# Overlapping the front of an attention block with the drain of a scan block, and weight scaling on GpSimd

## The chip, the cores and the metric

The kernel runs on one core of a Trainium2 chip. Its engines are named as in the profile: PE is TensorE (matmuls), ACT is ScalarE, DVE is VectorE, POOL is GpSimd, SP is SyncE, which issues nearly all DMAs. The metric is the device time of one launch in microseconds (us), the median over several runs.

## The reference

The input is 32 sequences of 256 tokens and 128 features. Two blocks follow each other, each a mixer and a feed-forward part with a residual and a layer norm behind either:

```python
x = _layernorm(x + _L0_attn_ref(x, ...))   # block 0: scan
x = _layernorm(x + _L0_ffn_ref(x, ...))
x = _layernorm(x + _L1_attn_ref(x, ...))   # block 1: attention
x = _layernorm(x + _L1_ffn_ref(x, ...))

# block 0's mixer
x_proj, res = split(x @ W_in.T)
xc = silu(conv_b + sum(conv_w[:, k] * xp[:, k:k + L, :] for k in range(4)))
delta = softplus(xc @ W_dt.T + b_dt)
h = exp(delta * A) * h + delta * Bp * xc      # 16 states, over the tokens
x_ssm = sum(h * Cp) + xc * Dp
return x_ssm * silu(res) @ W_out.T

# feed-forward, both blocks: ternary weights, a scale per output
h = silu(_tlin(x, w1_w, w1_s)) * _tlin(x, w2_w, w2_s)
h = gelu(_tlin(h, h1_w, h1_s)); h = gelu(_tlin(h, h2_w, h2_s))
return _tlin(h, w3_w, w3_s)

# block 1's mixer: 16 heads of 64, 4 memory keys and values in front
q = l2norm(q); k = l2norm(k)
dots = einsum('bhid,bhjd->bhij', q, k) * 10
dots = einsum('hg,bgij->bhij', W_pre_th, dots)
dots = where(causal, mask_value, dots)
vk = top_k(dots, 64)[0][..., -1:]
dots = where(dots < vk, mask_value, dots)
attn = einsum('hg,bgij->bhij', W_post_th, softmax(dots))
out = einsum('bhij,bhjd->bhid', attn, v) * head_scale_params
return (out * sigmoid(x @ Wg + bg)) @ Wo
```

## The kernel before

The program has two phases, one function each, and every engine's instructions are written out in one function per engine (`sync`, `tensor`, `scalar`, `vector`, `gpsimd`). Engines wait for each other on semaphores alone; the order on an engine is the order in which the Python loops emit it.

**Block 0** (`mixer_phase`, called first) is a software pipeline over SEQS + 5 = 37 periods. In period p the engines work on the projection, convolution and scan of sequence p and p - 1, the norm of p - 2, the feed-forward input products (w1, w2) and h1 of n = p - 3, h2 of m = p - 4, and w3 with the second norm (`nb`) of l = p - 5. Sixteen states t of a scan are sixteen `tensor_tensor_scan` on DVE (L921), each followed by a sum into y (L931), with other DVE work set between them at numbered t (LATE is 13). When a sequence's second norm is finished SP stores it to `x_mid` in HBM. PE writes h1 as 16 matmuls out of `f_a`, h2 as 16 out of `f_b` (both L363), w3 as 4 out of `f_c` (L400).

The feed-forward weights are ternary, with a scale per output. `scale_ins` (L143) multiplies w1 and w2 (128 x 512 each) and `scale_hidden` (L149) h1 and h2 (128 x 2048 each) by rows of scales. DVE calls them for block 0 (`f0`) in periods 1 and 2 at t = LATE (L995, L1002), and for block 1 (`f1`) in period 34. The scales come in one tile each, `w_f0rows` and `w_f1rows`. SP loads block 0's feed-forward weights (seven DMAs, `weights0_in`) behind the first sequence and block 1's (`weights1_in`) in period 1.

**Block 1** (`attention_phase`) is a pipeline over SEQS + 3 periods of 128 beats, ordered by tables of beats (`PE_K`, `PE_SCORE0`, `PE_PREMIX`, and so on for each engine). For one sequence b: key pieces `k_piece` (four matmuls of 512 columns for two token halves t and two feature halves), their squares on ACT, a reciprocal root of the norms by a guess on ACT and steps on POOL (`Root`), the transposes of the keys (`k_turn`, eight per token half) and their copies on ACT (`k_keep`); query pieces `q_piece`, squares, sums (`q_sum`), the turned norms (`q_turn`), clipped on DVE (`q_clip`), guess on ACT (`q_guess`), steps on POOL. Then the scores: block of queries 0 (`blk` 0, 132 keys wide) in 6 pieces and block 1 (260 keys) in 16, written by PE into three banks and copied by ACT with the query's scale into the tile `SN` (`s_keep`). SP stores `SN` to HBM (`stage`) and reads it back with 8 queries times 16 heads on the partitions into `T8` (`regroup`), because the heads must be mixed by a matmul. PE does that (`premix`, L1403), ACT copies it back (`t_keep`, L1607), POOL masks it (`hide`), and DVE ranks: eight values at a time, MAX8 and MATCH_REPLACE8, until the 64th largest is known. The ranking of one sequence is by far the largest work of DVE, 1.6 of its 3.4 ms.

Four rows of V per sequence belong to the last tokens of it (`tails`): their inputs are loaded together by one DMA into `x_tail` (in the tile `gate`), and two matmuls of 512 columns and two copies make them, ahead of the very first premix.

**Between the blocks** stands a barrier. For the first sequence of block 1 the keys are made in periods 34 and 35 and the queries in 36 and behind the loop, all inside `mixer_phase`. At the end of it PE, ACT, DVE and POOL each wait for `nb.normed` of the last sequence and raise their semaphore of `mixed_end`; each engine begins `attention_phase` by waiting for all four. Behind the barrier POOL clears `T8`, `V2` and the `AT` tiles by memsets, SP loads `x_tail`, and PE and ACT begin period -1 of the tables with the scores of sequence 0, into which the tables set the first premixes and the keys of sequence 1.

## Time and profile before

| | us |
|---|---|
| three runs, median | 3636.32 |
| lowest, highest | 3629.79, 3643.66 |
| the profiled execution | 3643.09 |
| its span in the trace | 3641.8 |

The granted TensorE clock was 0.981 of full over the span. Busy time of each engine, as a share of the span: PE 3402.0 us (93%), DVE 3429.3 (94%), ACT 3094.4 (85%), POOL 1742.1 (48%). The page cuts the span into 40 slices of 91 us: POOL is at 0 tenths for the first nine of them, which are block 0, and DVE is below 9 in four: the first, the two around the end of block 0, and the last. DMA moves 85 GB/s in the tenth slice, the one between the blocks, and 8 to 14 in block 0 behind the first. "Busy" is an average over stages with different limits, so each place that the change touches is read by itself: a window of the trace gives each engine's busy time in a stretch, a timeline gives single instructions with their start, and what ended the idle time before them stands in brackets.

### The profile page before, as it was taken

Reading aid. Unit: us, or ns where it says so; the run is one execution under the profiler, and the core shown is the slowest. Engines: PE = TensorE matmul, PEld = TensorE weight load, DVE = VectorE, ACT = ScalarE, POOL = GpSimd, SP = SyncE. Lnnn points to the kernel's source line nnn. Section 1 sums busy time; section 2 is a strip of 40 time slices with the busy share of each in tenths; the row PEclk is TensorE's granted clock in tenths of the full one; section 3 lists DMA queues with packets and bytes.
Section 4 is the critical chain, followed back from the end, with each engine's and each line's share of the span. In section 5 each row is a group of like instructions: output and inputs, shape, how many; then the busy total and the mean of one; then the engine's idle time right before and its main releaser. Section 6 shows DMA issues by size and latency. Waiting matters only on the chain.

```text
span 3641.8 us, 78829 instructions
## 1 busy us (share of the span) xinstructions
PE 3402.0 (93%) x19351; PEld 2539.4 (70%) x19351; DVE 3429.3 (94%) x18632; ACT 3094.4 (85%) x10837; POOL 1742.1 (48%) x3670
## 2 busy tenths in 40 slices
PE   4999999996999999999999999999999999999987
PEld 2888888873666666666666666666666666676665
DVE  7999999945999999999999999999999999999993
ACT  5888888856899898999999898998889989889863
POOL 0000000004666666666666666666666666666663
PEclk9999999997899999999999999999999999999998
DMA  3000000003222222222222222222222222222210
GB/s 132 11 14 13 13 13 13 10 8 85 68 74 71 76 83 66 65 65 65 67 65 65 73 70 71 74 69 76 77 73 66 65 65 65 67 65 65 73 55 4
DMA packets 254142, 210.76 MB, mean 58 GB/s; under 512 B 78000, under 2 KB 234736, under 8 KB 252912
## 3 DMA queue, kind: packets, MB, share of 16 engines
q1 hardware_dynamic: 253680, 205.70, 18.2%
q8 instruction: 155, 2.54, 0.3%
q14 instruction: 307, 2.51, 0.2%
HBM read 93.97 MB, written 111.67 MB: 56 GB/s over the span
## 4 chain that ended last, share of the span: by engine, by line
PE 64%; DVE 15%; ACT 14%; issue 3%; POOL 2%; DMA 0%; SPq 0%; DVEq 0%; ACTq 0%; POOLq 0%
PE bank L363 12%; PE bank L221 8%; PE bank L1415 5%; DVE W L1807 5%; PE bank L1403 5%; PE bank L1388 4%; DVE last L1829 3%; PE bank L331 3%; PE bank L1446 3%; PE bank L195 3%; PE bank L453 3%; PE bank L1480 3%; ACT SN L1599 3%; PE bank L1460 2%; PE bank L1419 2%
## 5 line engine op out<-in xcount | busy, mean ns | idle before, releaser
L1807 DVE MATCH_REPLACE8 W<-last,W 128x130 f32<-128x130 f32 (+18 forms) x3456 | 871.0, 259 | 0.0
L1829 DVE MAX8 last<-W 128x8 f32<-128x130 f32 (+18 forms) x3456 | 762.0, 261 | 0.1
L1914 POOL TENSOR_SCALAR posts<-post,share 128x128 f32<-128x128 f32 x1024 | 366.0, 379 | 284.2 <-DVE share L1736 279.7
L1583 ACT ACTIVATE T<-T,peak 128x260 f32<-128x260 f32 (+15 forms) x1024 | 410.9, 409 | 4.2 <-POOL T L1965 3.0
L1599 ACT ACTIVATE SN<-bank,rq 128x260 f32<-128x260 f32 (+1 forms) x1024 | 357.9, 424 | 61.4 <-PE bank L1388 59.7
L1403 PE MATMUL bank<-T,pre 128*128 128x40 f32 (+15 forms) x1024 | 366.1, 440 | 14.1 <-ACT T L1607 9.8
L1415 PE MATMUL bank<-posts,T 128*128 128x128 f32 (+7 forms) x2048 | 311.9, 289 | 69.1 <-POOL posts L1914 60.8
L1965 POOL TENSOR_TENSOR T<-T,below 128x520 f32<-128x520 f32 (+12 forms) x416 | 360.8, 884 | 19.9 <-DVE below L1838 4.6
L1415 PEld LDWEIGHTS bank<-posts,T 128*128 128x128 f32 (+7 forms) x2048 | 249.4, 174 | 165.5 <-POOL posts L1914 89.7
L921 DVE TENSOR_TENSOR_SCAN hs<-dA,dx 128x256 f32<-128x256 f32 x512 | 348.5, 681 | 4.7 <-ACT dA L783 1.9
L1930 POOL TENSOR_TENSOR T<-T,w_mask 128x32 f32<-128x32 f32 x512 | 141.2, 279 | 415.9 <-ACT T L1607 413.5
L1388 PE MATMUL bank<-kT,qT 64*128 64x260 f32 (+1 forms) x2048 | 276.6, 374 | 43.2 <-ACT SN L1599 33.5
L522 POOL TENSOR_SCALAR k_sq<-k_sq 128x16 f32<-128x16 f32 x64 | 17.6, 275 | 571.5 <-DVE k_sq L535 522.1
L1403 PEld LDWEIGHTS bank<-T,pre 128*128 128x128 f32 x1024 | 169.5, 193 | 165.6 <-issue 87.0
L1955 POOL TENSOR_SCALAR below<-T,last 128x244 f32<-128x244 f32 (+3 forms) x256 | 269.2, 1051 | 32.3 <-DVE last L1827 8.9
L1807 DVE MATCH_VALUE_LOAD W<-last,W 128x8 f32 x3456 | 260.9, 76 | 0.0
L221 PE MATMUL bank<-f_b,w_f1h 128*128 128x256 f32 x1024 | 248.6, 386 | 5.7 <-ACT f_b L233 5.7
L1607 ACT ACTIVATE T<-bank 128x40 f32<-128x40 f32 (+15 forms) x512 | 208.0, 406 | 50.2 <-PE bank L1403 47.9
L1552 ACT ACT_TABLE_LOAD x192 | 246.3, 1283 | 4.6 <-POOLq L1081 1.1
L221 PE MATMUL bank<-f_a,w_f1h 128*128 128x256 f32 x1024 | 247.7, 385 | 0.0
L783 ACT ACTIVATE dA<-delta,neg_a 128x256 f32<-128x256 f32 x512 | 235.8, 499 | 8.7 <-DVE delta L1048 8.6
L1388 PEld LDWEIGHTS bank<-kT,qT 64*128 64x128 f32 x2048 | 146.8, 191 | 136.7 <-ACT SN L1599 76.1
(243 smaller groups left out, 9571.9 us busy)
## 6 DMA issues: line engine op xcount, KB each, us to landing
scores_by_token<-SN SPq DMA_DIRECT2D x64, 520.0 KB, 3.0
scores_by_token<-SN SPq DMA_DIRECT2D x64, 396.0 KB, 3.6
scores_by_token<-SN SPq DMA_DIRECT2D x32, 780.0 KB, 3.3
scores_by_token<-SN SPq DMA_DIRECT2D x32, 264.0 KB, 2.7
scores_by_token<-SN SPq DMA_DIRECT2D x32, 260.0 KB, 2.3
T<-scores_by_token SPq DMA_DIRECT2D x32, 244.0 KB, 2.9
T<-scores_by_token SPq DMA_DIRECT2D x32, 228.0 KB, 3.1
T<-scores_by_token SPq DMA_DIRECT2D x32, 212.0 KB, 4.0
```

What stands on the lines that cost most here:

```text
L221: last = pe.matmul(o[:, (m % 2) * SEQ:(m % 2 + 1) * SEQ], self.w[layer][:, c, m * P:(m + 1) * P], src[:, c, :], start=c == 0, stop=c == HC ...
L363: last = pe.matmul(o[:, (m % 2) * SEQ:(m % 2 + 1) * SEQ], self.w[layer][:, c, m * P:(m + 1) * P], src[:, c, :], start=c == 0, stop=c == HC ...
L921: dve.tensor_tensor_scan(hs[j % NH][:], dA[j % ND][:], dx[b % 2][:], 0.0, ALU.mult, ALU.add).then_inc(scanned, 1)
L1388: last = pe.matmul(FRONT[(n + half) % 3][:, j * w:(j + 1) * w], qT[rows, even // 2, blk * P:(blk + 1) * P], kT[rows, even // 2, 0:w], star ...
L1403: pe.matmul(MIX[:, 0:pair.shape[-1]], pre[:], pair, start=True, stop=True).then_inc(premixed, 1)
L1415: return pe.matmul(at0[0:m, j * P:(j + 1) * P], scores(b, QUAD[i][j], 0, m), posts[(n + j) % NP][:], start=True, stop=True)
L1583: act.activation(one, one, ACT.Exp, bias=peak[k % 2][:, j:j + 1], accum_out=total[k % 4][:, j:j + 1]).then_inc(e_made, 1)
L1599: last = act.activation(SN[:, h, 0:w], FRONT[n % 3][:, j * w:(j + 1) * w], ACT.Copy, scale=rq[:, c:c + 1])
L1807: dve.match_replace(both[:, s, at:to], best[n], both[:, s, at:to], LOWEST).then_inc(ranked, 1)
L1829: dve.max(best[n], both[:, s, at:to]).then_inc(ranked, 1)
L1914: pool.tensor_scalar(posts[(4 * k + j) % NP][:], post[:], share[k % 2][:, j:j + 1], 1.0, ALU.mult, ALU.mult).then_inc(posts_made, 1)
L1965: pool.tensor_tensor(x, x, out, ALU.add).then_inc(dropped, 1)
```

## The change

Four things are changed.

1. `scale_ins` and `scale_hidden` are called by POOL, for both blocks, one set behind the other at the start of its program, as soon as the weights are in. The scales of both blocks are loaded into parts of `SN`, which is free until block 1; the two tiles for them are gone.
2. Keys and queries of the first sequence are made earlier: the first token half's keys at the end of period 33, the second half's ahead of h1 in period 34, the first half's transposes behind h1 of period 34, the queries in period 35. The scores of sequence 0 follow directly behind the last norm in period 36, all 22 pieces in a row, and SP's store of them likewise. `score`, `s_keep` and `stage` become methods of `Front` for it.
3. The barrier is taken apart: no `mixed_end`. PE makes the keys of sequence 1 and then the premixes of sequence 0, in a written order `FIRST`, and only then waits for `nb.normed`; ACT likewise; DVE waits for `nb.normed` at its start; POOL clears `T8` behind the last `na.normed`, and the rest behind `nb.normed` and the stores of `x_mid`.
4. The tails move to the first premix of sequence 1, with their input in `x_d`.

The diff, cut to what matters:

```diff
-def scale_ins(dve, w, rows, scaled):
+def scale_ins(pool, w, rows, scaled):
...
+        self.SN = room.sb("SN", [P, HEADS, KEYS])
+        by_row = self.SN[:].rearrange("p h n -> p (h n)")
+        self.f_rows = [by_row[:, n * 4 * HID:(n + 1) * 4 * HID].rearrange("p (k n) -> p k n", k=4) for n in range(2)]
...
# mixer_phase, sync
-                sp.dma_start(f1_rows[:], d["f1rows"]).then_inc(sh.weights1_in, 16)
+                sp.dma_start(sh.f_rows[1], d["f1rows"]).then_inc(sh.weights1_in, 16)
+            if p == LAST:
+                front.stage(sp, 0, 0)
# mixer_phase, tensor
-            if p == KEYS_A:
-                pe.wait_ge(f1.folded, 2)
-                front.k_piece(pe, 0, 0, 0)
-                front.k_piece(pe, 0, 0, 1)
-            if p == LAST:
-                front.q_piece(pe, 0, 0)
-                front.q_piece(pe, 0, 1)
-                front.k_turn(pe, 0, 1, 0)
...
+            if p == KEYS + 1:
+                front.k_piece(pe, 0, 1, 0)
+                front.k_piece(pe, 0, 1, 1)
             for k in range(HC):
                 if k == VAR_A and seq(o):
                     na.pe_var(pe, o)
...
                 if seq(n):
                     f0.pe_h1(pe, n, k)
+            if p == KEYS:
+                pe.wait_ge(f1.folded, 2)
+                front.k_piece(pe, 0, 0, 0)
+                pe.wait_ge(na.normed, SEQS)
+                front.k_piece(pe, 0, 0, 1)
+            if p == KEYS + 1:
+                front.k_turn(pe, 0, 0, 0)
+                front.k_turn(pe, 0, 0, 1)
+            if p == KEYS + 2:
+                front.k_turn(pe, 0, 1, 0)
+                front.k_turn(pe, 0, 1, 1)
+                for c2 in range(2, IC // 2):
+                    front.q_sum(pe, 0, c2 - 2)
+                    front.q_piece(pe, 0, c2)
...
+                front.q_turn(pe, 0)
+        for piece in range(0, len(S_PIECES[0]), 2):
+            front.score(pe, 0, 0, piece)
+        for piece in range(0, len(S_PIECES[1]), 2):
+            front.score(pe, 0, 1, piece)
-        pe.wait_ge(nb.normed, SEQS)
-        pe.sem_inc(sh.mixed_end[0], 1)
# mixer_phase, scalar
+            if p == LAST:
+                front.q_guess(act, 0)
# mixer_phase, vector
-                    scale_ins(dve, f0.w, f0.w["rows"], f0.scaled)
-                if p == 2 and t == LATE:
-                    scale_hidden(dve, f0.w, f0.w["rows"], f0.scaled)
-                if p == SEQS + 2 and t == 0:
-                    dve.wait_ge(sh.weights1_in, sh.WEIGHTS1)
-                    scale_ins(dve, sh.f1.w, f1_rows, sh.f1.scaled)
-                    scale_hidden(dve, sh.f1.w, f1_rows, sh.f1.scaled)
# mixer_phase, gpsimd
+        pool.wait_ge(sh.weights0_in, WEIGHTS0)
+        scale_ins(pool, f0.w, f0.w["rows"], f0.scaled)
+        scale_hidden(pool, f0.w, f0.w["rows"], f0.scaled)
+        pool.wait_ge(sh.weights1_in, sh.WEIGHTS1)
+        scale_ins(pool, f1.w, sh.f_rows[1], f1.scaled)
+        scale_hidden(pool, f1.w, sh.f_rows[1], f1.scaled)
# attention_phase
+    FIRST = [(0, k) for k in range(6)] + [x for k in range(QUADS) for x in ((1, k), (0, k + 6)) if x[1] < QUADS]
...
     def tensor(pe):
-        for s in sh.mixed_end[1:]:
-            pe.wait_ge(s, 1)
...
+        for f in range(2):
+            front.k_piece(pe, 1, 0, f)
+        pe.wait_ge(sh.pre_ready, 1)
+        for blk, k in FIRST:
+            premix(0, blk, k)
+        pe.wait_ge(sh.nb.normed, SEQS)
...
     def scalar(act):
-        for s in sh.mixed_end:
-            act.wait_ge(s, 1)
...
+        for f in range(2):
+            front.k_square(act, 1, 0, f)
+        for blk, k in FIRST:
+            t_keep(0, blk, k)
+        act.wait_ge(sh.nb.normed, SEQS)
...
     def vector(dve):
-        for s in sh.mixed_end:
-            dve.wait_ge(s, 1)
+        dve.wait_ge(sh.nb.normed, SEQS)
...
     def gpsimd(pool):
+        pool.wait_ge(sh.na.normed, SEQS)
+        pool.memset(T8[0][:], 0.0).then_inc(zeroed, 1)
+        pool.memset(T8[1][:], 0.0)
+        pool.wait_ge(sh.nb.normed, SEQS)
```

How it moves the instructions is shown at three places. A row is one instruction or a run of equal ones (x and their number), with its source line, output and inputs.

POOL at the start of its program, where `pre`, `post` are the tiles for the mixing weights and `mkv` the norms of the memory keys. Before:

```order
L1073 MEMSET pre 128x128
L1074 MEMSET post 128x128
L84 ISA
L84 TENSOR_TENSOR mkv<-mkv 64x1
L86 TENSOR_TENSOR mkv<-mkv 64x1
```

Now:

```order
L1128 MEMSET pre 128x128
L1129 MEMSET post 128x128
L146 ISA
L146 TENSOR_TENSOR w_f0w<-w_f0w,SN 128x512 x2
L153 TENSOR_TENSOR w_f0h<-w_f0h,SN 128x2048 x2
L146 TENSOR_TENSOR w_f1w<-w_f1w,SN 128x512 x2
L153 TENSOR_TENSOR w_f1h<-w_f1h,SN 128x2048 x2
L84 TENSOR_TENSOR mkv<-mkv 64x1
```

Eight products have come in between the clearing of `post` and the root of the memory keys' norms; two of 512 and two of 2048 elements for each block.

PE in the last two periods of block 0, around the last h1 (the 16 matmuls out of `f_a`, of sequence 31) and h2 (out of `f_b`). `w_wk,xb` are key pieces, `w_ident,ktok` transposes of keys, `xb,w_wq` queries. Before:

```order
L726 MATMUL bank<-x_a,w_cenmat 128x256
L432 MATMUL bank<-w_wk,xb 128x512 x2
L363 MATMUL bank<-f_b,w_f0h 128x256 x4
L273 MATMUL bank<-nb_sq,w_meanmat 128x256
L363 MATMUL bank<-f_b,w_f0h 128x256 x8
L441 MATMUL bank<-w_ident,ktok 128x128 x4
L363 MATMUL bank<-f_b,w_f0h 128x256 x4
L441 MATMUL bank<-w_ident,ktok 128x128 x4
L453 MATMUL bank<-xb,w_wq 128x256 x4
L441 MATMUL bank<-w_ident,ktok 128x128 x4
```

Now:

```order
L435 MATMUL bank<-w_wk,xb 128x512 x2
L363 MATMUL bank<-f_a,w_f0h 128x256 x16
L444 MATMUL bank<-w_ident,ktok 128x128 x8
L400 MATMUL bank<-f_c,w3c 128x256 x4
L771 MATMUL bank<-x_a,w_cenmat 128x256
L456 MATMUL bank<-xb,w_wq 128x256 x4
L363 MATMUL bank<-f_b,w_f0h 128x256 x4
L273 MATMUL bank<-nb_sq,w_meanmat 128x256
L363 MATMUL bank<-f_b,w_f0h 128x256 x12
L444 MATMUL bank<-w_ident,ktok 128x128 x8
```

The key pieces of the second token half have moved ahead of the last h1, the transposes of the first half directly behind it, in one run of eight, where they stood between the matmuls of the last h2; the queries have moved ahead of that h2.

PE from the turned query norms (`w_stack,qn`) to the premixes (`T_0,pre`). `kT,qT` are scores, `f_c,w3c` is w3 of the last sequence, `w_wv,gate` the tails. Before:

```order
L472 MATMUL bank<-w_stack,qn 128x16 x2
L1388 MATMUL bank<-kT,qT 128x132 x16
L1388 MATMUL bank<-kT,qT 128x260 x2
L1370 MATMUL bank<-w_wv,gate 128x512 x2
L1403 MATMUL bank<-T_0,pre 128x40
L1388 MATMUL bank<-kT,qT 128x260 x2
L1403 MATMUL bank<-T_0,pre 128x72
L1388 MATMUL bank<-kT,qT 128x260 x2
L1403 MATMUL bank<-T_0,pre 128x104
L1403 MATMUL bank<-T_0,pre 128x136
L1388 MATMUL bank<-kT,qT 128x260 x4
L1403 MATMUL bank<-T_0,pre 128x168
```

Now:

```order
L475 MATMUL bank<-w_stack,qn 128x16 x2
L400 MATMUL bank<-f_c,w3c 128x256 x4
L771 MATMUL bank<-x_a,w_cenmat 128x256
L273 MATMUL bank<-nb_sq,w_meanmat 128x256
L570 MATMUL bank<-kT,qT 128x132 x16
L570 MATMUL bank<-kT,qT 128x260 x16
L435 MATMUL bank<-w_wk,xb 128x512 x2
L1441 MATMUL bank<-T_0,pre 128x40
...
L1441 MATMUL bank<-T_0,pre 128x200
L1441 MATMUL bank<-T_0,pre 128x512
L1441 MATMUL bank<-T_0,pre 128x232
```

w3 and the norm of the last sequence, which stood ahead of the query norms, now stand between them and the scores; the scores are in one run; the tails and the premixes between them are gone; and the keys of sequence 1 stand ahead of the first premix. The premix of 512 columns is the first of block 1 (260 keys), on which the ranking waits.

## Rows read from the trace of the kernel before

**Rows 1.** Windows of all engines; columns: window, length, busy time and instructions, PEclk, DMA.

```profile
36.00:38.00 2.00, 0.00 (x0) 0.00 (x0) 2.00 (x6) 1.98 (x5) 0.00 (x0) 1.00 0.04 16
...
50.00:75.00 25.00, 10.30 (x28) 7.19 (x28) 24.96 (x49) 15.62 (x36) 0.00 (x0) 0.96 0.03 6
...
820.00:830.00 10.00, 7.17 (x39) 4.53 (x38) 0.00 (x0) 6.32 (x19) 10.00 (x4) 0.53 0.68 130
...
860.00:870.00 10.00, 4.25 (x12) 1.66 (x12) 9.93 (x54) 6.84 (x46) 2.68 (x5) 0.92 0.01 2
```

**Rows 2.** The chain in order of time, around 112 us: start, length, what.

```profile
112.31 0.61 DVE w3c L1001
112.97 1.99 PE bank L400 x8
```

**Rows 3.** Timeline of DVE in the start-up: start, length, instruction.

```profile
24.67 0.42 DVE L1021 SCALAR_TENSOR_TENSOR sp_err<-sp_u,sp_e 128x256 f32<-128x256 f32 x1
...
44.75 1.28 DVE L146 TENSOR_TENSOR w_f0w<-w_f0w,w_f0rows 128x512 f32<-128x512 f32 x2
...
65.79 4.48 DVE L153 TENSOR_TENSOR w_f0h<-w_f0h,w_f0rows 128x2048 f32<-128x2048 f32 x2
```

**Rows 4.** Groups of POOL by form: busy us, mean ns of one | idle before.

```profile
L1965 POOL TENSOR_TENSOR T<-T,below 128x264 f32<-128x264 f32 x32 | 23.9, 745 | 0.0
...
L1976 POOL TENSOR_TENSOR gate<-gate,f_b 128x512 f32<-128x512 f32 x64 | 80.4, 1277 | 44.5 <-ACT f_b L1650 44.5
```

**Rows 5.** Timeline of SP's queue: the issue of block 0's last feed-forward load.

```profile
8.30 1.50 SPq L326 DMA_DIRECT2D w_f0s<-in_f0s  x1
```

**Rows 6.** DMA issues: KB each, median us from issue to landing.

```profile
w_f0s<-in_f0s SPq DMA_DIRECT2D x1, 0.5 KB, 11.5
```

**Rows 7.** Timeline of POOL and DVE from 3514 to 3516.5 us.

```profile
3514.56 1.27 POOL L1976 TENSOR_TENSOR gate<-gate,f_b 128x512 f32<-128x512 f32 x1 [0.28 <-ACT f_b L1650]
...
3514.66 1.43 DVE L1784 TENSOR_TENSOR W<-T 128x228 f32<-128x228 f32 x1
...
3516.01 0.38 DVE L1787 TENSOR_TENSOR W<-T 128x228 f32<-128x228 f32 x1
```

**Rows 8.** Timeline of DVE and POOL from 274.9 to 277.2 us.

```profile
275.72 0.69 DVE L921 TENSOR_TENSOR_SCAN hs<-dA,dx 128x256 f32<-128x256 f32 x1 [0.32 <-DVE dx L1054]
...
275.86 0.54 POOL L88 TENSOR_SCALAR mkv<-mkv 64x1 f32<-64x1 f32 x1
```

**Rows 9.** Timeline from the drain of block 0 to the first ranking instruction.

```profile
771.55 1.88 PE L432 MATMUL bank<-w_wk,xb 128*128 128x512 f32 x4
...
792.22 1.28 ACT L812 ACT_TABLE_LOAD   x1
...
801.56 0.58 ACT L501 ACTIVATE kT<-bank 128x512 f32<-128x512 f32 x1
...
810.40 0.43 ACT L269 ACTIVATE nb_sq<-bank 128x256 f32<-128x256 f32 x1
...
812.80 0.42 ACT L287 ACTIVATE nb_rs<-nb_rs 128x256 f32<-128x256 f32 x1
...
818.08 0.23 ACT L78 ACTIVATE q_t<-q_sq 128x32 f32<-128x32 f32 x1 [0.93 <-DVE q_sq L550]
...
820.97 1.68 ACT L1599 ACTIVATE SN<-bank,rq 128x132 f32<-128x132 f32 x6
...
837.96 0.82 PE L1403 MATMUL bank<-T,pre 128*128 128x136 f32 x2 [0.39 <-ACT T L1607]
...
844.34 1.24 PE L1388 MATMUL bank<-kT,qT 64*128 64x260 f32 x4 [0.56 <-ACT SN L1599]
...
847.41 0.85 ACT L1599 ACTIVATE SN<-bank,rq 128x260 f32<-128x260 f32 x2 [0.95 <-PE bank L1388]
...
849.76 1.91 PE L432 MATMUL bank<-w_wk,xb 128*128 128x512 f32 x2
...
854.45 1.22 PE L1403 MATMUL bank<-T,pre 128*128 128x512 f32 x2 [0.19 <-DMA T<-scores_by_token]
...
856.91 0.43 DVE L1784 TENSOR_TENSOR W<-T 128x260 f32<-128x260 f32 x1 [21.94 <-POOL T L1930]
```

More of the change, by code:

```diff
@@ L578, in __init__ @@
         self.mid_out = room.sems("mid_out", 2)
-        self.mixed_end = [room.sem(f"mixer_{e}_end") for e in ("pe", "act", "dve", "pool")]
     def load_block1(self, queue):
@@ L1149, in attention_phase @@
     x_d = room.sbs("x_d", [P, SEQ], 2)
+    x_tail = x_d[0][:, 0:SEQS * MEM]
     hh = sh.hh
@@ L1329, in regroup @@
                     sp.dma_start(side_by_side(b, g), rows[:, :, 0:width(g)]).then_inc(regrouped[blk][k // 2], 16)
+        sp.wait_ge(zeroed, 1)
+        regroup(0, 0)
+        front.stage(sp, 0, 1)
+        regroup(0, 1)
+        for b in range(2):
+            sp.wait_ge(sh.mid_out[b], 16 * (SEQS // 2))
+        sp.dma_start(x_tail.rearrange("p (b t) -> p b t", b=SEQS), tails).then_inc(tail_in, 16)
         for p in range(PERIODS):
             f, r, a = p, p - 1, p - 2
-            if seq(f + 1):
+            if f and seq(f + 1):
                 b = f + 1
@@ L1522, in tensor @@
                 for n in range(3):
-                    if (b := whose(p, t, PE_SCORE0[n], 0)) is not None:
-                        score(b, 0, 2 * n)
+                    if b := whose(p, t, PE_SCORE0[n], 0):
+                        front.score(pe, b, 0, 2 * n)
                 if (b := whose(p, t, PE_W3, 2)) is not None:
@@ L1528, in tensor @@
                 for n in range(8):
-                    if (b := whose(p, t, PE_SCORE1[n], 0)) is not None:
-                        score(b, 1, 2 * n)
+                    if b := whose(p, t, PE_SCORE1[n], 0):
+                        front.score(pe, b, 1, 2 * n)
                 if (b := whose(p, t, PE_VAR2, 2)) is not None:
```

323 lines of the change are left out of this document (157 added, 166 removed).

## The prediction

> **What bounds the kernel now.** I read the windows first, then the chain of waits in order of time, and then the timelines of the two places that the change touches. Block 0 has a start-up. From 50 us on VectorE (DVE) is busy for 24.96 of 25 us while TensorE (PE) is busy for 10.30 [rows 1]. The chain runs through DVE until 112.3 us, its last piece there the copy of w3's folded weights, and from the first w3 at 112.97 on it is PE that sets the pace [rows 2]. So up to 112 us a microsecond on DVE is a microsecond of the end; from there to the end of block 0 DVE time costs nothing unless it exceeds PE's small lead. Block 1 is bound by DVE's ranking from its first instruction on: in 860 to 870 DVE is busy 9.93 of 10 us [rows 1], and the first ranking instruction starts at 856.91 after waiting 21.94 us for masked scores [rows 9]. So the second number that counts is when that instruction starts. What happens before it, on PE, ScalarE (ACT) and the queues, counts only if it moves it. All else of block 1 is the same work in the same order.
>
> **Part 1: the scaling leaves DVE.** DVE loses 1.28 us (two 128x512) and 4.48 us (two 128x2048) [rows 3]. Both stand in the DVE-bound start-up: a gain of 5.8. The block 1 weights, scaled by DVE in the drain when it had little to do, gain nothing.
>
> **Part 2: the same scaling on GpSimd (POOL).** No row has a 128x2048 product on POOL. Two-input POOL products of 264 and 512 elements take 745 and 1277 ns [rows 4], 2.15 ns per further element, which gives 745 + 1784 x 2.15 = 4.6 us for 2048. In proportion to the longer row it would be 4 x 1277 = 5.1 us, and I keep that as the upper end; the lower end is DVE's own 2.24. One set of four is 2 x 1.28 + 2 x 4.57 = 11.7 us. POOL waits for all seven loads of block 0; the last, s3, is issued at 8.30 and lands 11.5 us later [rows 5, 6], at 19.8. The first set is done at 31.5, well before PE takes up h1, at the end of period 3: that it is scaled on DVE as late as 65.79 now [rows 3] does no harm either. The second set waits for block 1's weights, whose transfers end within 36 to 38 us [rows 1]; it runs from about 37 to 49.
>
> By itself that is free, since POOL has nothing else to do. But does it hold DVE up? A DVE product of two SBUF tiles that started 0.10 us after a two-input POOL product took 1.43 us, to just beyond POOL's end, where its twin took 0.38 [rows 7]. The other way round, a POOL instruction of one element, issued inside a DVE scan, lasted 0.54 us, to the scan's end [rows 8]. So scans too hold what POOL needs. Nearly every DVE instruction of the start-up reads two SBUF tiles (scan: dA and dx; sum: hs and y; taps: xp and taps). I take it that each of them waits for the POOL product in progress, and that DVE gets one instruction in between two products, which costs POOL, not DVE. The bounds: no hold of scans and sums, 0 us; a hold of the full set, 11.7 us. The rows are nearest to the full hold.
>
> The Trainium skill ("SBUF — State Buffer", Who interferes with whom) says that a VectorE instruction with two SBUF inputs and a GpSimd instruction that reads SBUF exclude each other for a whole instruction, whichever comes second waiting. This speaks against the change and would give the full hold; by the rows alone, which show a waiting DVE only for TENSOR_TENSOR, the hold of scans and sums would still be open. On the product the trace agrees (1.43 against 0.38 us).
>
> First set: DVE's second two-input instruction after 20 us starts at 24.67 now [rows 3]; the first waits for h1 and this one for h2, until 31.5. The delay is 6.8 us, and passes on, since the convolution, delta and the first scan hang on it. Second set: DVE is fully busy from 29 us on, and loses 11.7. Start-up: 6.8 + 11.7 - 5.8 = **+12.7 us**. Steady block 0 is the same.
>
> **Part 3: keys, queries and roots move into the drain.** In the order, the eight transposes of token half 0 come directly behind the last h1 on PE. The second of the two groups waits for ACT to copy the first, and ACT must first finish the last GELU (which waits for that same h1), load a table (1.28 us) and take the root guess (0.4), then copy (0.58) [rows 9]: PE waits some 2.4 us that it did not before. The key and query matmuls only change place. Then ACT copies key group 1,1 before the last feed-forward GELU, and only after that GELU come the last two query pieces, so q_turn is at about 816.0, some 1.2 earlier than now (the clipped norms leave DVE just ahead of 818.08 [rows 9]). Here a new dependency bites: q_turn now comes before w3 of sequence 31, and ACT guesses the query roots after the whole norm of sequence 31. Twelve 256-column matmuls (w3, centring, variance) take some 2.8 us, and ACT's squares to the second guess took 810.40 to 813.22 [rows 9]. The guess of the query roots starts at about 821.3 where it started at 818.08, and four POOL steps later the first score copy is at 823.2, not 820.97 [rows 9]. That is 2.2 us **later**.
>
> **Part 4: scores without interruption.** From there block 0's scores take some 6.1 us, as they do now. Block 1's 8 pairs are no longer cut up by the tails' matmuls (3.5 us of PE) and the first premixes. A pair took 1.24 us on PE and 0.56 of wait [rows 9], 1.8, so 829 (823.2 and 6.1) + 8 x 1.8 + 0.4 = 843.8 for the last copy, where it was 848.3 [rows 9]. The transfers follow as before (6.2 us from the last copy to the first premix of block 1), landing at 850. T8's memsets run from 823 on POOL and are done before the first regroup (about 833): hidden by the store of the scores.
>
> **Part 5: what takes their place.** Now the key matmuls of sequence 1 stand between scores and premix. They need the banks of the last scores, so they start at 843.8: two groups of 1.91 us [rows 9], overlapping to 847.3. ACT loads a table (1.28) beside that and then squares the second piece (8 squares with their sums, 1.7) before it copies the first premix: 849.1. Five more small premixes follow before the one that the ranking needs. Each handoff from ACT to PE and back took 0.82 + 0.39 = 1.2 us at the low clock [rows 9]. The clock was granted in full again after the dense key matmuls of the kernel before (0.53 over 820 to 830, 0.92 over 860 to 870 [rows 1]); matmuls then take half (1.88 us for four, not two [rows 9]), so I take 0.8 each: 853.1. The premix of block 1 then leads to the first ranking instruction as at 854.45 to 856.91 [rows 9], 2.5 us, with the full clock 2.1: 855.2. The scores arrive 4.5 us earlier, and three of those are given back. Part 3 to 5: **-1.7 us** (bounds: -4.9 if only the transfers counted, +2.8 at the low clock throughout).
>
> The tails' product moves to period 1 (two matmuls, two copies, about 4 us). There attention and feed-forward of the sequences behind are still missing, so PE and ACT have room: 0. One barrier became several waits; the waits that remain are for work long finished: 0.
>
> **Sum.** 12.7 - 1.7 = +11.0 us. The profiled execution took 3643.09 us (span 3641.8), which becomes 3654; it stood 6.8 above the median of the three runs (3636.32), so the median becomes **3647**. Three runs spread over 14 us. About 0.5% (18.2 us) is what a measurement of this kernel can tell from no change, so this is a forecast of no change by that bound, on the slow side.
>
> **The rivals.**
> (a) POOL does not hold scans and sums. For it: only a DVE product is seen waiting in the trace. Against: a scan is seen holding POOL [rows 8]. Start-up -5.8, in all -7.5: 3629.
> (b) Slower than before by more than the bound: the granted clock stays at its low level from the last h2 to the first ranking. Its place is PE's w3, variance and the premixes. By the key matmuls (0.47 against 0.94 us) twelve matmuls cost 2.8 us more, and five premixes 1.7: the ranking starts at 859.7, +2.8. With POOL's upper price (12.8 us a set, first set to 32.6) the start-up is +14.9, in all +17.7: 3654. It passes 0.5% if the ranking starts later than 860.2 (counted without the start-up's shift). For it: 0.53 over 820 to 830. Against: the clock was full in 860 to 870.
> (c) The change does what its words say and more: the premixes of block 0's scores cost nothing and only transfers count. Start -4.9, with the hold +7.8: 3644; without it -10.7: 3626. Against it stands PE's written order.
>
> **How the numbers follow.** Forecast 0.62, (a) 0.18, (b) 0.12, (c) 0.08. The range that holds 8 in 10 takes in (a) at 3629 with a little of the spread and (b) with some: 3627 to 3656; the forecast's own is 3641 to 3654. Slower by over 0.5%: most of (b) and the upper end of the forecast, 0.12. Faster by over 0.5% needs 18 us, more than (a) and (c) together give: 0.04. Within: 0.84.
>
> **What would show it.** In the start-up: four POOL products from about 20 and four from about 37 us, DVE instructions of 4 to 5 us between them, the w3 of sequence 0 at about 125 instead of 112.97. If scans keep 0.68 us beside POOL, (a) is right. In the drain: a PE wait of some 2 us between the two transpose groups, the first score copy 2 us later and the first ranking instruction 1 to 2 us earlier, both counted from the same w3. Wrong would be: block 1 periods of another length than 84.8 us, or a ranking that starts 5 us earlier or later than I say.

## The result, and the profile after

The changed kernel takes 3665.22 us (median of 4 runs, 3662.34 to 3669.02); the kernel before, measured again beside it, 3638.48 (4 runs). The ratio is 1.0083, with a 95% interval of 1.0071 to 1.0096: about 30 us slower by the ratio, 27 by the medians. The forecast was 3647, with a range up to 3656.

The first place is the start-up. Timeline of POOL, then of DVE, in the kernel after (start, length, instruction, idle time before it):

```profile
20.07 2.49 POOL L146 TENSOR_TENSOR w_f0w<-w_f0w,SN 128x512 f32<-128x512 f32 x2 [18.81 <-DMA SN<-in_f0rows]
22.51 9.01 POOL L153 TENSOR_TENSOR w_f0h<-w_f0h,SN 128x2048 f32<-128x2048 f32 x2
38.02 2.95 POOL L146 TENSOR_TENSOR w_f1w<-w_f1w,SN 128x512 f32<-128x512 f32 x2 [6.50 <-DMA SN<-in_f1rows]
40.94 9.51 POOL L153 TENSOR_TENSOR w_f1h<-w_f1h,SN 128x2048 f32<-128x2048 f32 x2
```

```profile
24.41 2.76 DVE L1074 TENSOR_SCALAR sp_u<-sp_e 128x256 f32<-128x256 f32 x1 [13.44 <-ACT sp_e L902]
27.09 4.71 DVE L972 SCALAR_TENSOR_TENSOR taps<-xp,w_vec,taps 128x256 f32<-128x256 f32 x1
31.73 0.41 DVE L1077 SCALAR_TENSOR_TENSOR sp_err<-sp_u,sp_e 128x256 f32<-128x256 f32 x1
...
41.44 4.65 DVE L992 SCALAR_TENSOR_TENSOR y<-hs,bc,y 128x256 f32<-128x256 f32 x1
46.02 4.98 DVE L982 TENSOR_TENSOR_SCAN hs<-dA,dx 128x256 f32<-128x256 f32 x1
50.92 0.45 DVE L992 SCALAR_TENSOR_TENSOR y<-hs,bc,y 128x256 f32<-128x256 f32 x1
```

Each long POOL product has one DVE instruction beside it that ends when it ends: a sum of 4.65 us and a scan of 4.98, where the next sum takes 0.45. The chain in order of time shows what that came to:

```profile
125.09 0.61 DVE w3c L1063
125.74 1.99 PE bank L400 x8
```

The first w3 starts 12.8 us later than in [rows 2]. The windows say the same: in 50 to 75 us DVE is as full as in [rows 1] and PE is busy for 6.22 us, not 10.30. The second line here is the stretch after the key matmuls, for the place that follows:

```profile
50.00:75.00 25.00, 6.22 (x12) 3.52 (x12) 24.96 (x56) 16.48 (x39) 0.45 (x1) 1.00 0.03 6
...
862.00:872.00 10.00, 6.21 (x13) 3.07 (x14) 0.22 (x2) 2.84 (x15) 1.76 (x7) 0.58 0.71 149
```

The second place is the drain. Timeline of the kernel after, with the instructions that answer to [rows 9]:

```profile
805.90 0.60 PE L444 MATMUL bank<-w_ident,ktok 128*128 128x128 f32 x4
...
809.11 1.08 PE L444 MATMUL bank<-w_ident,ktok 128*128 128x128 f32 x4 [2.60 <-ACT kT L504]
809.98 3.06 PE L400 MATMUL bank<-f_c,w3c 128*128 128x256 f32 x8
...
835.62 0.21 ACT L78 ACTIVATE q_t<-q_sq 128x32 f32<-128x32 f32 x1
...
837.55 1.68 ACT L590 ACTIVATE SN<-bank,rq 128x132 f32<-128x132 f32 x6 [1.46 <-POOL rq L90]
...
856.26 0.85 ACT L590 ACTIVATE SN<-bank,rq 128x260 f32<-128x260 f32 x2 [0.95 <-PE bank L570]
...
857.25 3.38 PE L435 MATMUL bank<-w_wk,xb 128*128 128x512 f32 x4 [1.02 <-ACT SN L590]
...
868.94 2.05 PE L1441 MATMUL bank<-T,pre 128*128 128x512 f32 x2 [0.52 <-ACT T L1635]
...
871.98 0.43 DVE L1816 TENSOR_TENSOR W<-T 128x260 f32<-128x260 f32 x1 [8.53 <-POOL T L1951]
```

The wait of 2.60 us between the two groups of transposes was forecast (2.4); what stands behind it was not, and comes up again under the experiments. Counted from the first w3 of each kernel, the first score copy is 3.8 us late (711.8 against 708.0), the last one ends at 731.4 where it ended at 735.3, 3.9 early, and the first ranking instruction is 2.3 us late (746.24 against 743.94).

The third place is one that the forecast did not have. The first ranking instruction of sequence 1, in the kernel before and then in the one after:

```profile
941.58 0.43 DVE L1784 TENSOR_TENSOR W<-T 128x260 f32<-128x260 f32 x1 [0.35 <-POOL T L1930]
```

```profile
970.35 0.43 DVE L1816 TENSOR_TENSOR W<-T 128x260 f32<-128x260 f32 x1 [0.26 <-POOL T L1951]
```

From the first ranking to this the kernel before needed 84.7 us, the one after 98.4: 13.7 more. The waits of DVE in 871 to 973 us (us in total, times, the longest) name them, and in the kernel before none of the last three is there:

```profile
DVE W L1816 <- POOL T L1951: 8.8, 2, 8.5
DVE top L1883 <- issue: 6.0, 1, 6.0
DVE top L1883 <- POOL T L1986: 4.7, 1, 4.7
DVE below L1870 <- POOL T L1986: 3.7, 1, 3.7
```

What POOL did is in its timeline. `T<-T,w_mask` is the mask behind a premix; sixteen stand in a row, at the pace at which PE and ACT hand premixes to each other, and only then come the negated scores, the roots of sequence 1's keys, and the product on which the ranking waits:

```profile
871.70 0.25 POOL L1951 TENSOR_TENSOR T<-T,w_mask 128x32 f32<-128x32 f32 x1 [2.57 <-ACT T L1635]
...
889.24 0.25 POOL L1951 TENSOR_TENSOR T<-T,w_mask 128x32 f32<-128x32 f32 x1 [1.81 <-ACT T L1635]
891.10 0.25 POOL L1951 TENSOR_TENSOR T<-T,w_mask 128x32 f32<-128x32 f32 x1 [1.61 <-ACT T L1635]
891.32 0.25 POOL L1943 TENSOR_SCALAR neg<-T 128x68 f32<-128x68 f32 x1
...
894.08 1.28 POOL L1986 TENSOR_TENSOR T<-T,below 128x520 f32<-128x520 f32 x1
```

In the kernel before that product started at 866.84, 9.9 us behind the first ranking instruction and not 22.1, with eleven masks before it and the later ones behind it. So up to the ranking of sequence 1 the traces differ by 12.8 + 2.3 + 13.7 = 28.8 us. Behind that point they differ the other way: 2700.2 us to the end before, 2690.7 after. That stretch is not part of the change: over the fourteen profiled executions of this study it lies between 2686.8 and 2700.2 us, for the unchanged attention code too, and the profiled execution of the kernel before is the longest of them. Hence the spans differ by 19.2 us only, while the ratio of the runs says 30 (26 to 35 by its interval), and the 28.8 lies inside that.

### The profile page after: what moved, and what is told of

Its sections match the earlier page's. It is cut to its first block, busy times and chain, and to the rows that moved or that the text cites. A ratio compares the mean times of both kernels' runs of the same rounds, so it can differ in the third digit from the quotient of the medians.

```text
span 3661.0 us, 78820 instructions
## 1 busy us (share of the span) xinstructions
PE 3398.4 (93%) x19351; PEld 2531.6 (69%) x19351; DVE 3434.1 (94%) x18624; ACT 3094.6 (85%) x10837; POOL 1766.2 (48%) x3678
## 4 chain that ended last, share of the span: by engine, by line
PE 66%; ACT 16%; DVE 12%; issue 4%; POOL 2%; SPq 0%; DMA 0%; DVEq 0%; ACTq 0%; POOLq 0%
PE bank L363 12%; PE bank L221 8%; PE bank L1453 5%; PE bank L1441 5%; PE bank L570 5%; DVE W L1839 4%; PE bank L331 3%; PE bank L456 3%; PE bank L1484 3%; PE bank L195 3%; ACT SN L590 3%; PE bank L1518 3%; PE bank L1498 3%; DVE last L1861 3%; ACT sq L483 2%
## 5 line engine op out<-in xcount | busy, mean ns | idle before, releaser
L1441 PE MATMUL bank<-T,pre 128*128 128x488 f32 (+15 forms) x1024 | 369.7, 444 | 16.4 <-ACT T L1635 14.1
```

The source lines that it names most:

```text
L1441: pe.matmul(MIX[:, 0:pair.shape[-1]], pre[:], pair, start=True, stop=True).then_inc(premixed, 1)
```

## The experiments

The theory after the result had three parts: POOL's products hold DVE in the start-up (12.8 us); the list `FIRST` makes PE, ACT and POOL finish all sixteen premixes before they do what the ranking of sequence 0 needs next (13.7); the query guess and the small premixes delay the first ranking (2.3). The rivals were the moved loads and tiles, the barrier that is gone, and TensorE's clock. The table gives the stages of every profiled execution, from their timelines: the first scan, from there to the first w3, from there to the first ranking instruction, from there to that of sequence 1.

| kernel | first scan | to first w3 | to first ranking | first period |
|---|---|---|---|---|
| before | 29.19 | 83.78 | 743.94 | 84.67 |
| after | 36.25 | 89.49 | 746.24 | 98.37 |
| e1 | 34.86 | 89.49 | 746.26 | 88.82 |
| e2 | 28.06 | 83.78 | 746.23 | 98.38 |
| e3 | 36.97 | 89.63 | 742.35 | 86.00 |
| e4 | 36.93 | 79.09 | 742.27 | 85.84 |
| e5 | 34.72 | 89.50 | 744.64 | 85.42 |
| e6 | 34.89 | 89.45 | 739.47 | 88.23 |
| e7 | 29.80 | 83.79 | 753.16 | 85.76 |
| e8 | 27.72 | 91.31 | 741.98 | 85.74 |
| e9 | 28.13 | 80.18 | 736.18 | 91.60 |
| e10 | 30.63 | 81.23 | 742.01 | 84.67 |
| e11 | 29.01 | 80.78 | 742.41 | 85.06 |
| e12 | 28.35 | 83.96 | 743.66 | 84.67 |

Two things in it must be known before single microseconds are compared. The first sp_u, which hangs on the landing of the inputs, starts anywhere from 22.6 to 25.2 us in kernels whose DVE code is the same up to there, so the first scan is compared less closely than the rest. And the stretch from w3 to the ranking differs by steps of 1.6 or 1.7 us between executions of one code. Up to the last scan of block 0 there is none: it starts 633.3 to 633.4 us behind the first w3 in every execution but e7's. The steps lie in the drain, and two of them can be seen, each directly behind a wait of PE. The first stands 634.8 us behind the first w3 (644.7 in e7), where PE waits 2.03 us for DVE in all fourteen executions; behind that wait twelve of them show the granted clock at its lower level for a while and e10 and e12 do not. PE in the kernel after and in e12, over nearly the same ten microseconds (634 on; one window of each, the kernel after first):

```profile
760.00:770.00 10.00, 9.48 (x40) 8.30 (x41) 2.53 (x7) 3.27 (x6) 0.00 (x0) 0.83 0.00 0
```

```profile
746.00:756.00 10.00, 8.92 (x45) 8.00 (x46) 4.04 (x10) 3.82 (x7) 0.00 (x0) 1.00 0.00 0
```

The granted clock is 0.83 in one and 1.00 in the other; 0.17 of ten microseconds is 1.7. The second step stands behind the wait of 2.60 us between the transposes, which only kernels with the change's drain have. In the kernel after the eight matmuls of w3 behind it take 3.06 us (the row at 809.98 above); in e9 they take 1.89 behind the same wait:

```profile
791.67 0.63 PE L444 MATMUL bank<-w_ident,ktok 128*128 128x128 f32 x4 [2.60 <-ACT kT L504]
792.13 1.89 PE L400 MATMUL bank<-f_c,w3c 128*128 128x256 f32 x8
```

Of the eight kernels with that drain six show the step in their trace (after, e1, e2, e5, e6, e11) and two do not (e9, e12); the six with the old drain do not have the wait. So this one is in part a price of the change. Steps included, the stretch to the first ranking is 742.0 to 743.9 us in the five executions of the old drain (before, e3, e4, e8, e10; e3 lacks the scaling in period 34) and 743.7 to 746.3 in the four with the change's (after, e1, e2, e12). The 2.3 us between before and after are one pair out of these; the medians are 4.0 apart.

### e1: fewer premixes ahead

```diff
-    FIRST = [(0, k) for k in range(6)] + [x for k in range(QUADS) for x in ((1, k), (0, k + 6)) if x[1] < QUADS]
+    FIRST = [(0, k) for k in range(6)] + [(1, 0), (0, 6), (0, 7)] + [(1, k) for k in range(1, QUADS)]
+    HEAD = 7
...
-        for blk, k in FIRST:
+        for blk, k in FIRST[:HEAD]:
...
-                        if b := whose(p, t, PE_PREMIX[blk][k], 0):
+                        if (b := whose(p, t, PE_PREMIX[blk][k], 0)) is not None and (b or mixed_as(0, blk, k) >= HEAD):
```

> The changed kernel, but only the first seven premixes of sequence 0 are written ahead of the tables; the other nine stand at the beats that the tables give them, as in the kernel before. Theory (the list that writes all sixteen premixes ahead of everything holds back what POOL, ACT and PE owe to the first ranking): the first period of block 1 falls from 98.4 us to about 84.7, DVE's three waits of 4.7, 3.8 and 6.0 us go, and the whole is some 14 us faster than the changed kernel, about 13 slower than before. Rival (those waits come from the lost barrier or from TensorE's low clock, whatever the order): the period stays at 95 us or more and the time within 3 us of the changed kernel. Start-up (first w3 at 125.7) unchanged by either.

Measured: 3649.13 us, ratio to before 1.0037 (1.0024 to 1.0050), 16 us less than the changed kernel. The waits of DVE in 870 to 960 us:

```profile
DVE W L1817 <- POOL T L1952: 9.2, 2, 8.5
DVE share L1769 <- ACT T L1629: 3.3, 1, 3.3
```

The three waits are gone. The first period of the profiled execution is 88.8, not 84.7, by a wait of 3.3 us for ACT's exponentials; e5 and e12, with the same table, have 85.4 and 84.7, so this one belongs to the execution. e12 against e2 is the same edit with the scaling on DVE in both: 84.67 against 98.38. The order of the list is the cause; the lost barrier is not, since it is lost here too. TensorE's clock rose with the order: it was granted 0.67 in the 20 us behind the first ranking here (870.6 to 890.6) and 0.50 in the kernel after (872 to 892). How much of the 13.7 us passes through it no run separates.

### e2: scaling back on DVE

```diff
+                    scale_ins(dve, f0.w, f0.w["rows"], f0.scaled)
...
+                if p == 2 and t == LATE:
+                    scale_hidden(dve, f0.w, f0.w["rows"], f0.scaled)
+                if p == SEQS + 2 and t == 0:
+                    dve.wait_ge(sh.weights1_in, sh.WEIGHTS1)
+                    scale_ins(dve, sh.f1.w, sh.f_rows[1], sh.f1.scaled)
+                    scale_hidden(dve, sh.f1.w, sh.f_rows[1], sh.f1.scaled)
...
-        pool.wait_ge(sh.weights0_in, WEIGHTS0)
-        scale_ins(pool, f0.w, f0.w["rows"], f0.scaled)
-        scale_hidden(pool, f0.w, f0.w["rows"], f0.scaled)
-        pool.wait_ge(sh.weights1_in, sh.WEIGHTS1)
-        scale_ins(pool, f1.w, sh.f_rows[1], f1.scaled)
-        scale_hidden(pool, f1.w, sh.f_rows[1], f1.scaled)
```

> The changed kernel with all scaling back on DVE at its old places (block 0's in periods 1 and 2, block 1's in period 34); all else as changed. Theory (POOL's products hold DVE): the first w3 is back at 113.0 us instead of 125.7, 12.8 us faster than the changed kernel, about 15 us slower than before. Rival (the start-up is late because of the loads, whose order or target changed): the first w3 stays beyond 120. The first period of block 1 stays at 98.4 in both.

Measured: 3652.25 us, ratio 1.0041 (1.0027 to 1.0054). First scan to first w3 is 83.78, as before to the hundredth, first w3 at 111.84. The rows are still loaded into `SN`, so the loads' target is not the cause.

### e3 and e4: scaling on POOL in the kernel before, both sets, and the first alone

e3 is the reverse of e2's diff in the kernel before; e4 moves only the `f0` lines.

> The kernel before with only the scaling moved to POOL, both sets at the start as in the change, rows in their own tiles. Theory (hold): first w3 at 125.7 instead of 113.0, everything behind it unchanged, so 12.8 us slower than before, first period of block 1 at 84.7. Rival (loads or tiles of the change): within 3 us of before.

> The kernel before with only block 0's scaling on POOL (20 to 31.5 us), block 1's still on DVE in period 34. By the terms of the sum: the hold of the first set costs 6.8 and DVE is relieved of 5.8, first w3 at about 114.0, 1.0 us slower than before, which the times cannot tell from nothing. Rival (the first set costs its full 11.5 us): first w3 at about 118.7. Rival (DVE time in the start-up is not on the path): first w3 at 119.8.

Measured: e3 3652.47 us, ratio 1.0033 (1.0018 to 1.0049); first w3 at 126.60, 0.9 us later than in the kernel after, of which 0.7 is the input's landing (sp_u at 25.15, there at 24.41). e4 3640.29 us, ratio 1.0009 (0.9999 to 1.0018), which is not told apart from no change; first w3 at 116.02 with sp_u at 24.97. Of the 2.0 us beyond the 114.0 expected 0.9 is the later sp_u and 1.1 a relief smaller than forecast. Together they price the terms. From sp_u to the first scan 5.13 us became 11.96: the first set's hold is 6.8. From first scan to w3 e3 less e4 is 89.63 - 79.09 = 10.5: the second set's hold. Before less e4 is 83.78 - 79.09 = 4.7: the relief. 6.8 + 10.5 - 4.7 = 12.6. The relief is less than the 5.8 us of products taken off DVE because DVE then waits longer elsewhere. Waits of scans behind `dx` from 28 us to the first w3, before and then in e4:

```profile
DVE hs L921 <- DVE dx L1054: 0.8, 1, 0.8
DVE hs L921 <- DVE dx L1051: 1.7, 3, 0.8
```

That is 0.9 us more.

### e5 and e6: the query guess early, and the wide premix early

```diff
+            if p == LAST:
+                front.q_guess(act, 0)
             if seq(l):
                 nb.act_square(act, l)
```

e5 has this line order and e1's table. e6 adds:

```diff
+    FIRST = [(0, k) for k in range(4)] + [(1, 0)] + [(0, k) for k in range(4, 8)] + [(1, k) for k in range(1, QUADS)]
+    HEAD = 5
...
-        for f in range(2):
-            front.k_piece(pe, 1, 0, f)
...
-                    if (b := whose(p, t, PE_K[n], 0)) and (b > 1 or n >= 2):
+                    if b := whose(p, t, PE_K[n], 0):
```

> As e1_tables, and ACT guesses the roots of the query norms ahead of the last norm's squares instead of behind its second guess. In the changed kernel the guess begins at 835.62 and the first score copy at 837.55, 711.8 us behind the first w3. Theory (the guess was queued behind the norm): POOL's steps are done before the norm's guesses, the first copy then waits for those on ACT alone (they end at 835.7) and comes 1.8 us earlier, and with it the first ranking (746.2 behind the first w3 before, 744.4 now). Rival (the scores wait for PE's w3 and variance): no gain at all.

> As e5, and the wide premix that the first ranking needs comes fifth, behind four small ones, with the first keys of sequence 1 behind it at the beats of the tables (as in the kernel before). Theory (keys, their squares and the small premixes stood in the way, 857.2 to 869.7): the wide premix now waits for its transfer alone, lands some 7 us behind the last score copy, and the first ranking is about 5 us earlier than e5's, 739.5 behind the first w3 (743.9 in the kernel before); first period of block 1 still 84.7 to 86. Rival (the transfers set it anyway): under 1 us gained over e5.

Measured: e5 3649.39 us, ratio 1.0034 (1.0020 to 1.0048), no faster than e1 by the times; in the trace the first score copy comes 1.8 us earlier, as computed, and the ranking 1.6. e6 3647.65, ratio 1.0033 (1.0021 to 1.0044); the first ranking at 739.47, as computed, but the first period is 88.2 instead of 85.4, so 2.8 of the 5.2 us are given back, by waits for the second wide premix and for ACT.

### e7: block 1's scaling on POOL in the middle of block 0

```diff
-                if p == SEQS + 2 and t == 0:
-                    dve.wait_ge(sh.weights1_in, sh.WEIGHTS1)
-                    scale_ins(dve, sh.f1.w, f1_rows, sh.f1.scaled)
-                    scale_hidden(dve, sh.f1.w, f1_rows, sh.f1.scaled)
...
+        pool.wait_ge(na.normed, 10)
+        pool.wait_ge(sh.weights1_in, sh.WEIGHTS1)
+        scale_ins(pool, f1.w, f1_rows, f1.scaled)
+        scale_hidden(pool, f1.w, f1_rows, f1.scaled)
```

> The kernel before with only block 1's scaling on POOL, begun when ten sequences have their first norm, so in the steady, PE-bound part of block 0 (about 330 us). DVE is busy for 526.6 of 540 us there. Theory (the hold is the same 10.5 to 12 us, and DVE leads PE by little): most of it comes through to PE, the first ranking is 6 to 12 us late, start-up unchanged at 113. Rival (PE sets the pace, so a held DVE costs nothing there): within 2 us of before.

Measured: 3645.57 us, ratio 1.0029 (1.0019 to 1.0038), first ranking 9.2 us late; at the last scan of block 0, ahead of the drain and its steps, it was 9.9. Window of 260 to 300 us, and PE's longest wait in 200 to 740 us, where the kernel before has none:

```profile
260.00:300.00 40.00, 33.79 (x143) 28.71 (x143) 39.72 (x67) 26.78 (x62) 14.21 (x8) 0.91 0.03 11
```

```profile
PE bank L746 <- DVE z L1009: 6.2, 1, 6.2
```

PE waits 6.2 us for DVE, and the clock that it is granted falls to 0.91 in that window, where the kernel before has 1.00: the wait is followed by a slower stretch besides. So PE's lead in the steady part does not cover a hold either.

### e8: long POOL instructions with one input

```diff
+        pool.wait_ge(sh.weights1_in, sh.WEIGHTS1)
+        for k in ("w1", "w2", "h1", "h2"):
+            pool.tensor_scalar(sh.f1.w[k][:], sh.f1.w[k][:], 1.0, None, ALU.mult).then_inc(passed, 1)
```

> The kernel before, all scaling on DVE as it was, and POOL multiplies block 1's weights by 1.0 (one input, a scalar: two of 512 and two of 2048 elements) as soon as they are in, at about 37 us; no result changes. Theory (POOL holds DVE by its two SBUF inputs): one-input instructions of POOL hold nothing, DVE's scans keep 0.68 us beside them and the first w3 stays at 113. Rival (any long POOL instruction on SBUF holds DVE): scans of several us beside them, the first w3 late by about POOL's busy time there.

Measured: 3642.63 us, ratio 1.0018 (1.0009 to 1.0028). Neither theory holds. Timeline of POOL, then DVE:

```profile
36.23 3.30 POOL L1079 TENSOR_SCALAR w_f1w<-w_f1w 128x512 f32<-128x512 f32 x2 [34.97 <-DMA w_f1rows<-in_f1rows]
39.51 11.02 POOL L1079 TENSOR_SCALAR w_f1h<-w_f1h 128x2048 f32<-128x2048 f32 x2
```

```profile
39.84 4.11 DVE L922 TENSOR_TENSOR_SCAN hs<-dA,dx 128x256 f32<-128x256 f32 x1
43.88 0.45 DVE L932 SCALAR_TENSOR_TENSOR y<-hs,bc,y 128x256 f32<-128x256 f32 x1
44.25 0.68 DVE L922 TENSOR_TENSOR_SCAN hs<-dA,dx 128x256 f32<-128x256 f32 x1
44.85 0.45 DVE L932 SCALAR_TENSOR_TENSOR y<-hs,bc,y 128x256 f32<-128x256 f32 x1
45.23 4.11 DVE L922 TENSOR_TENSOR_SCAN hs<-dA,dx 128x256 f32<-128x256 f32 x1
```

Each POOL instruction of 2048 elements takes 5.5 us and holds one scan for 3.4 of them, then lets three DVE instructions start and run at their usual length before the next one holds again. The first w3 comes 7.5 us late (91.31 against 83.78) for 14.3 us of POOL. One input holds less than two, but it holds.

### e9 to e12: what is left, alone and joined

e12 is e1 and e2 together, the change's drain alone. e10 is the kernel before with h1 and h2 of block 0 scaled by DVE in its idle time at the start:

```diff
-                pe.wait_ge(f0.scaled, 2)
+                pe.wait_ge(f0.scaled, 4)
...
-                if p == 2 and t == LATE:
-                    scale_hidden(dve, f0.w, f0.w["rows"], f0.scaled)
...
+                if p == 0 and t == PLUS:
+                    dve.wait_ge(sh.weights0_in, WEIGHTS0)
+                    scale_hidden(dve, f0.w, f0.w["rows"], f0.scaled)
```

e9 is the changed kernel with that, the rest of the scaling on DVE at its old places, e6's list and keys, and HEAD = 10. e11 is e9 with the keys of sequence 1 ahead of the premixes again and HEAD = 7.

> The changed kernel with both found costs undone: scaling on DVE at its old places and nine premixes at the beats of the tables (e1 and e2 together). What is left is the change's drain. Theory (the terms add): first w3 at 113 less what the inputs land earlier, first ranking 746.2 behind it (743.9 before), first period 85 to 86: 2 to 4 us slower than before. Rival (the overlap of the drain gains once the other two are gone): faster than before.

> The kernel before with only this: DVE scales h1 and h2 of block 0 ahead of the first sp_u. Theory: 3.5 to 4.7 us faster than before, all of it in the start-up. Rival (the loads land too late): within 1 us of before. Against e9 it gives the drain's own part.

> What the runs so far leave of the change: its drain with the query guess early and ten premixes ahead (four small ones, the wide one of the first ranking, four small, the second wide one), the rest and the first keys of sequence 1 at the beats of the tables; all scaling on DVE, block 1's in period 34, block 0's h1 and h2 (4.5 us) set ahead of the first sp_u, into the idle time in which DVE waits for ACT at the start (until 24 us). Theory: first w3 3.5 to 4.7 us earlier after the first landing of the inputs (first scan to first w3 79.3, not 83.8, and the first scan at most 0.8 later), first ranking 739.5 behind the first w3 (743.9 before), first period of block 1 at 85 to 86: 7 to 9 us faster than before. Rival (the loads land too late, and sp_u waits for the products): start-up as before, 4 us faster. Rival (the first period gives the drain's gain back, as e6's 88.2): 4 us less.

> As e9, but the first keys of sequence 1 ahead of all premixes again, as in the change, then four small premixes, the wide one, two small ones; the rest by the tables. The question is whether two chains set the first period: the wide premix (e9: first ranking 736.2 behind the first w3, then a wait of 5.6 us for ACT's peaks, which came 771.0 behind it), and the keys of sequence 1, whose scaling and copies stand ahead of those peaks on ACT. Theory (two chains): first ranking later than e9's, at 741.8, the 5.6 us wait gone, first period 85 to 86 instead of 91.6, so the second period begins 827 behind the first w3, where e9 had 827.8 and before 828.6: 1 us over e9, 4 us faster than before. Rival (the wait for peaks hangs on premixes alone): the wait stays and the second period begins at 832 or later.

| | median us | ratio to before | 95% interval |
|---|---|---|---|
| e12 | 3638.44 | 1.0006 | 0.9996 to 1.0015 |
| e10 | 3632.22 | 0.9996 | 0.9987 to 1.0004 |
| e9 | 3634.48 | 0.9999 | 0.9989 to 1.0009 |
| e11 | 3631.24 | 0.9981 | 0.9972 to 0.9990 |

e12: by the times the drain that is left cannot be told from the kernel before; the median is 2.8 us over, inside the 2 to 4 expected, but the interval takes in no difference as well. Its trace has neither of the two steps, and its first ranking is 0.3 us earlier than in the kernel before, which has one. e10: from first scan to w3 it is 2.6 us shorter (83.78 to 81.23), but the products ran from 21.09 to 25.50 with sp_u directly behind them, so part of that is paid ahead of the first scan, and the times do not tell the rest from nothing (3.5 to 4.7 us were expected). e9 was expected to be 7 to 9 us faster than before and is not faster by the times. In its trace sequence 1 begins at 936.10 us, 5.5 earlier than before; the median of its twelve runs does not show it, and why stays open. In e9 the ranking starts 7.8 us earlier than before and the first period takes 91.6 us. Its waits of DVE in 844 to 940 us:

```profile
DVE W L1815 <- POOL T L1950: 7.7, 2, 7.0
DVE top L1882 <- issue: 5.6, 1, 5.6
```

`top` waits for ACT's peaks, and these stand behind the scaled keys of sequence 1 and their copies in ACT's order. e11 makes those keys first; its waits in 852 to 940 us:

```profile
DVE W L1819 <- POOL T L1954: 6.3, 2, 5.9
DVE top L1886 <- issue: 1.2, 1, 1.2
```

The ranking starts 6 us later than in e9 and sequence 1 begins 827.5 us behind the first w3 (827 was computed; e9 has 827.8, before 828.6). So two chains set the first period, and moving either ahead of the other gains little: 0.3 us between these two traces, of which e11's has the step behind the 2.60 us wait and e9's has not, so that like for like e11's order may be worth up to 2 us more. e11 is the only kernel here that is measured faster than before, by 0.2% (6.9 us by the ratio, 4 expected).

## Why the prediction was wrong

**Start-up: right, +12.7 forecast, +12.8 measured** (0.35 of it is a first sp_u that started at 24.41 and not at 24.06). The POOL products took 1.25 and 4.5 us (1.28 and 4.57 said), and the first sp_err moved from 24.67 to 31.73 (31.5 said). The parts were each a little off and cancelled: the second hold was 10.5, not 11.7, because the four DVE instructions beside it, 12.8 us together, would have taken 2.3 by themselves, which I had not set off; the relief was 4.7, not 5.8, because scans waited 0.9 us more once the products were gone (e4). That the sum comes out within 0.4 us is luck in so far as these two errors have opposite signs. Rival (a), that scans and sums are not held, is refuted by the two rows of 4.65 and 4.98 us and by e2, e3 and e4. The Trainium skill ("SBUF — State Buffer", Who interferes with whom) gave the full hold for two inputs, and the trace agrees (4.98 against 0.68 us). For a POOL instruction with one input e8 does not bear out a hold for its whole length: the scan beside the first 5.5 us instruction was through at 43.95, 1.1 us before it.

**Drain to the first ranking: wrong in sign, -1.7 forecast, +2.3 measured.** Over all pairs of executions with the old and the changed drain it is -0.3 to +4.3, so never near the forecast. Times of the kernel after that stand beside forecast ones are counted less the start-up's shift of 12.8 us; windows are in its own time. The PE wait was 2.6 us (2.4 said). The first score copy was 3.8 us late and not 2.2: the wait was forecast, the low clock behind it, 1.6 to 1.7 us, was not. The scores then ran faster than said, and the last copy's end was 844.3 (843.8 said). ACT was done with the squares at 849.7 (849.1 said). The term that failed most is "so I take 0.8 each", the small premixes at the full clock. From the first premix copy to the start of the premix of block 1 it took 6.4 us and not 4.0, the premixes starting 0.9 to 1.6 us apart at a granted clock of 0.58 in 862 to 872, and the last step took 3.0 us and not 2.1. 0.6, 2.4 and 0.9 are the miss of 4.0 (855.2 said, 859.2 measured). Rival (b) said 859.7, and its mechanism holds for the premixes. Its larger term, 2.8 us for w3, centring and variance of sequence 31 at the low clock, did not come: the granted clock was 1.00 from 814 to 839, and the eight matmuls of w3 took 1.97 us. That its number is so near is luck. The clock of 0.92 in 860 to 870 that I held against it [rows 1] was that of a stretch in which PE also ran the tables' work; here PE handed the small premixes to and fro with ACT and had nothing between them. That this is why the clock stayed low is the likely reading; no run tests it by itself.

**Block 1: the step that failed.** "All else of block 1 is the same work in the same order" left out 13.7 us. It is the same work, but not in the same order: the sixteen premixes of sequence 0 stand in one block on PE, ACT and POOL, ahead of the first ranking's own products, peaks and masks. I had asked of `FIRST` only when the seventh premix comes, and not what is queued behind the other nine on POOL. Without this term the other two, 12.8 + 2.3 = 15.1 us, would have given 3651 to 3654, inside the range. e1 shows it by taking the order back. So does e12 against e2. That the barrier went cost nothing that a run shows.

**Tails, barrier, transfers.** The tails' product in period 1 showed no wait: the second period of the kernel after is 85.05 us, where it was 85.02. Rival (c), that only transfers count, is refuted: the premix of block 1 waited for ACT in the kernel after. Of the kernels with the change's drain only e6 and e9 have it wait for its transfer (1.5 us), where four and not six small premixes stand ahead of it and the keys behind it.

## What to carry over

A list of work written ahead of a schedule must be read on every engine for what it is ahead of, not only for what it contains: an in-order engine that hardly works (POOL was busy for 2.8 us in 872 to 892) can hold the busiest one. An engine with nothing to do is no free place for work if it shares what the busy engine needs: price the move by the busy engine's instructions beside it. And when a bound chain is shortened, ask at once for the next one; here it was less than 8 us behind. Last, a difference of 2 us between two traces is little where executions of one code differ by steps of 1.6 us: more traces of both sides, or a row that shows the step, must stand beside it.

## What was unexpected of the hardware

A one-input POOL instruction in SBUF holds a DVE scan for 3.4 us of its 5.5 and then no more (e8); the 512-element ones (1.67 us) held DVE for about 0.3 us each. A one-input DVE instruction, TENSOR_SCALAR of 128x256 from SBUF, was held as well by a two-input POOL product: 2.76 us at 24.41, where it takes 0.29. And a pause of 6.2 us on PE in the middle of a dense stretch was followed by a lower granted clock (0.91 over 40 us), so that it cost more than itself: 9.9 us at the last scan of block 0. Shorter waits were followed by the low clock in some executions and not in others: one of 2.03 us in twelve of fourteen, one of 2.60 us in six of eight, at 1.6 or 1.7 us each.
